# A non-local attention block on one NeuronCore: image loop written out, products placed at block ends, and the turned diagonal tiles of blocks 2 to 5 multiplied as halves

## The chip, the core and the metric

The kernel runs on one NeuronCore of a Trainium2 chip. TensorE (PE, its weight loads PEld) multiplies, VectorE (DVE), ScalarE (ACT) and GpSimd (POOL) work on tiles, and SyncE (SP) issues the DMAs. The engines run side by side and wait for each other on semaphores. The metric is the device time of one execution in microseconds; three executions of the kernel before gave 2091.82, 2092.5 and 2095.53 us, the median is 2092.5 us.

## The reference

```python
x = x + L(gn(x), g_w, g_b, W_w, W_b, gamma, beta)   # x: 4 images, 256 channels, 64 x 64
# inside L, for one image, with v = gn(x) as 256 x 4096:
g_x  = g_w @ v + g_b                    # 128 x 4096
f    = v.T @ v                          # 4096 x 4096, symmetric
attn = softmax(f, axis=-1)
y    = attn @ g_x.T                     # 4096 x 128
wy   = W_w @ y.T + W_b                  # 256 x 4096
# then a batch norm of wy over all four images, plus v
```

`gn` is a group norm with 32 groups. All of it is float32.

## The kernel before, in words

**Blocks and tiles.** The 4096 positions of an image are cut into NB = 8 blocks of 512. f is symmetric, so only the chunks (j, c) with c >= j are multiplied (`multiply`, L1280 to L1282): the operands are split into a high and a low part (`xh`, `xl`, in a rounded type called fp32r), and a product of 128 rows by 512 columns is six matmuls. VectorE takes it out of PSUM with the row maxima (L1067), and takes column maxima into `colmax` (L1075). A chunk stays in a slot of `ring` (or in a part of `fy_c` and `fy_d`) and is spilled to DRAM for later use.

**One step.** A block j of outputs is the sum over 32 tiles of 128 by 512, so an image has 8 x 32 = 256 steps, numbered 0 to 255; step 32 j + i is tile i of block j. A "right" tile comes from chunks (j, c) of the block itself. Its exponential is taken with the row maxima (ACT, L863), it is turned by four transposes of TensorE (`turn`, L1333, done two steps ahead) into one of two banks, cast to a high half `phi` by ScalarE (`split_hi`, L904, 3 buffers), its low half `plo` is made by VectorE (`split_lo`, L1098, 2 buffers), and TensorE multiplies with three fp32r matmuls (`attend`, L1361 to L1363). A "left" tile is a part of an earlier chunk that needs no turn: POOL subtracts the spread row maxima `maxrow` (L784), ScalarE takes the exponential (L883), VectorE adds it to the column sum `lacc` (L1109, L1113), and TensorE multiplies it in one full float32 matmul (L1357; the trace has two records for it). In blocks 1 to 6 the four tiles of the diagonal chunk (j, j) are taken as left tiles as well, straight from `ring`: the "turned diagonal tiles". Right tiles are the only ones that are split.

**Order.** Every engine has its own instruction stream, written by `step(b, s, ...)` for the steps in turn. In one step TensorE first turns the tile of step s + 2, then makes the products that `PRODUCT_STEP` puts at s, then multiplies tile s; after that come small transposes and projections. ScalarE makes in step s the exponential of the left tile of step s + 3, the high half for step s + 2, and then the exponentials of right tiles. VectorE makes the low half of step s, then sums, then takes the products. POOL goes through the left tiles in order, as far ahead as its data allow; at a block's start it waits for `maxrow` (L874 on ScalarE). `PRODUCTS_FROM` says at which step the products of block j begin. `plan_products` spreads them over a number of steps from there; the steps at which the maxima of a block are merged (`MERGE_STEP`) follow from the last product. From step `NEXT_AT` on, the first products of the next image are made, which need the next image's `xl` (POOL, L755).

**Images.** Images 0 to 3 follow each other. Step 12 of image 0 to step 11 of image 3 are one hardware loop over three rounds on every engine (`Fori`, on TensorE at L1483), in which each wait compares with a number computed from the loop's register; image 3 from step 12 on is written out.

Of the kernel before, what the change touches and what calls it, by code (L numbers as in the profile page):

```python
# [25 lines left out]
F32 = mybir.dt.float32  # L26
# [48 lines left out]
PRODUCTS_FROM = {j: (j - 1) * TPB for j in range(1, NB)} | {6: 5 * TPB - 8, 7: 5 * TPB + 8}  # L75
# [53 lines left out]
FULL = range(1, NB)  # L129
SPLIT = [p for p in range(TILES) if not (tile(p)[3] and p // TPB in FULL)]  # L130
# [37 lines left out]
def plan_products():  # L168
# [3 lines left out]
    for j in range(1, NB):  # L172
        n = T * (NB - j)
        steps = range(PRODUCTS_FROM[j], PRODUCTS_FROM[j] + {1: 22, 2: 19, 3: 18, 4: 18, 5: 18, 6: 2 * n, 7: 2 * n}[j])
# [85 lines left out]
NEXT_AT, NEXT_TO = XN_STEP[0] + 5, TILES - 18  # L260
# [145 lines left out]

def nonlocal_block(nc, x, wg, bg, ww, vec, out):
# [5 lines left out]
    with ExitStack() as ctx:  # L413
# [128 lines left out]
        lo_made = sem("lo_made")  # L542
        left_added = sem("left_added")
# [54 lines left out]
        def pool_subs(b, w):  # L598

            n = b * NLEFT + w  # L600
            return n - sum(v < w for v in VSUBS) if isinstance(b, int) and b == B - 1 else n
# [17 lines left out]
        def y_home(b, j):  # L619

            return colmax[:, j, :] if isinstance(b, int) and j < NB - 1 else yn[:, :]
# [6 lines left out]
        def _(sp):  # L628
# [94 lines left out]
            with sp.Fori(0, B - 1) as b:  # L723
# [21 lines left out]
        def _(pool):  # L745
# [16 lines left out]

            def image(b, more):
                for c in range(len(NEXT_G), NB):
                    make_gl(b, c)
                for w in range(NLEFT):
# [8 lines left out]

                    if not more and w in VSUBS:
                        continue
# [28 lines left out]
            with pool.Fori(0, B - 1) as b:  # L806
                image(b, True)
# [5 lines left out]
        def _(act):  # L813
# [53 lines left out]
            def take_maxrow(b, j):  # L867
# [4 lines left out]
                if isinstance(b, int) and b == B - 1 and VSUBS[0] < LEFT_OF[j][0]:  # L872
# [3 lines left out]
            def exp_left(b, p):  # L876

                w = LEFT_NO[p]
                if isinstance(b, int) and b == B - 1 and w in VSUBS:
# [31 lines left out]
            def take_inverse(b, j):  # L911

                act.wait_ge(inverse_spread, b * NB + j + 1)
                if j > 0:
                    if isinstance(b, int):
# [60 lines left out]
            with act.Fori(0, B - 1) as b:  # L976
# [27 lines left out]
        def _(dve):  # L1004
# [145 lines left out]
            def step(b, p, more, tail=False, first=False):  # L1150
                j, i = divmod(p, TPB)
                if p in SPLIT_NO:
                    split_lo(b, p, first)
# [55 lines left out]
            with dve.Fori(0, B - 1) as b:  # L1209
# [47 lines left out]
        def _(pe):  # L1257
            last_image = B - 1
# [60 lines left out]
            def turn(b, p, first=False):  # L1319
# [7 lines left out]
                if n >= 2:  # L1327
                    pe.wait_ge(lo_made, b * NSPLIT + SPLIT_NO[IN_PSUM[n - 2]] + 1)
                elif not first:
                    pe.wait_ge(lo_made, b * NSPLIT + SPLIT_NO[IN_PSUM[n - 2]] + 1 - NSPLIT)  # L1330
# [6 lines left out]
            def attend(b, p, first=False):  # L1337
# [6 lines left out]
                if p in SPLIT_NO:  # L1344
                    pe.wait_ge(lo_made, b * NSPLIT + SPLIT_NO[p] + 1)
                else:
                    w = LEFT_NO[p]
                    if w in LEFT_OF[j][:2]:
# [208 lines left out]
```

## Time and profile before

| what | value |
|---|---|
| median of three executions | 2092.5 us |
| the profiled execution's own time | 2091.74 us |
| its span, first to last instruction | 2090.0 us |
| TensorE busy | 2027.0 us, 97% |
| VectorE, ScalarE, GpSimd busy | 1543.7, 1110.8, 788.9 us |
| mean granted TensorE clock | 0.999 of full speed |
| TensorE idle before L1333, released by VectorE's low half | 15.1 us in 30 places |

A row of the timeline reads: start in us, length in us, engine, line, operation, output<-input, count, and in brackets the idle time before it and what ended it. Matmuls overlap, so the distance between the starts of two rows is what one costs, and the length of a row is not. Image 1's steps run from about 574.3 to 1072.0 us of the span and image 2's to 1571.5 us.

### The profile page before, as it was taken

What the parts mean: (1) busy time and instruction counts of PE and PEld (TensorE: products, weight loads), DVE (VectorE), ACT (ScalarE), POOL (GpSimd) and SP (SyncE); (2) the same over time, 40 slices, a digit from 0 to 9 for tenths busy, and PEclk for the clock granted to TensorE, in tenths of its full rate; (3) what the DMA queues carried; (4) which work ended last, traced back from release to release, by engine and by line L of the source; (5) the groups of instructions that cost most, each with busy time, mean ns of one, the idle gap of its engine ahead of it and who ended that gap; (6) DMA issues with size and microseconds to landing.
All of it is one profiled execution on the core that took longest, in us unless ns stands there. A gap on an engine that the chain in (4) does not pass through costs nothing.

```text
span 2090.0 us, 32328 instructions
## 1 busy us (share of the span) xinstructions
PE 2027.0 (97%) x9348; PEld 1453.2 (70%) x9348; DVE 1543.7 (74%) x3113; ACT 1110.8 (53%) x2312; POOL 788.9 (38%) x608
## 2 busy tenths in 40 slices
PE   5999999999999999999999999999999999999998
PEld 4787777666688777766678777766668877776443
DVE  5777777877777777787777677787777677777777
ACT  4345555566545445547553555546645544554656
POOL 4001233469601123458820122246970202344740
PEclk9999999999999999999999999999999999999999
DMA  3222334556411333565622223455551132346988
GB/s 126 112 90 87 106 117 126 177 165 207 163 68 72 121 101 104 160 201 158 215 82 82 82 94 129 131 177 161 186 187 66 66 121 94 99 131 200 338 297 346
DMA packets 107542, 300.29 MB, mean 144 GB/s; under 512 B 11488, under 2 KB 11872, under 8 KB 93536
## 3 DMA queue, kind: packets, MB, share of 16 engines
q1 hardware_dynamic: 107360, 298.11, 41.9%
q8 instruction: 84, 1.38, 0.3%
q14 instruction: 98, 0.80, 0.1%
HBM read 157.55 MB, written 140.51 MB: 143 GB/s over the span
## 4 chain that ended last, share of the span: by engine, by line
PE 75%; issue 8%; POOL 7%; DVE 4%; ACT 4%; DMA 1%; SPq 0%; ACTq 0%; DVEq 0%; POOLq 0%
PE bank L1357 13%; PE bank L1280 11%; PE bank L1282 11%; PE bank L1281 11%; PE bank L1333 8%; PE bank L1361 4%; PE bank L1363 4%; PE bank L1362 4%; PE bank L1516 3%; POOL fy_c L784 3%; POOL fy_d L784 3%; PE bank L1427 2%; ACT ring L863 2%; DVE plo L1098 1%; POOL xl L755 1%
## 5 line engine op out<-in xcount | busy, mean ns | idle before, releaser
L904 ACT CAST phi<-bank 128x512 fp32r<-128x512 f32 x480 | 281.3, 586 | 697.8 <-PE bank L1333 696.0
L1067 DVE TENSOR_SCALAR_CACHE_REDUCE ring<-bank 128x512 f32<-128x512 f32 x560 | 385.7, 690 | 269.0 <-PE bank L1282 197.5
L1280 PE MATMUL bank<-xh 128*128 128x512 f32 (+3 forms) x1152 | 513.8, 446 | 10.5 <-POOL xl L755 10.2
L1098 DVE TENSOR_TENSOR plo<-bank,phi 128x512 fp32r<-128x512 f32 x480 | 329.8, 687 | 153.4 <-ACT phi L904 107.3
L1282 PE MATMUL bank<-xh,xl 128*128 128x512 f32 (+3 forms) x1152 | 436.3, 379 | 0.0
L1281 PE MATMUL bank<-xl,xh 128*128 128x512 f32 (+3 forms) x1152 | 433.4, 376 | 0.0
L863 ACT ACTIVATE ring<-ring,nmax 128x512 f32<-128x512 f32 x464 | 334.2, 722 | 1.3
L784 POOL TENSOR_TENSOR fy_d<-fy_d,maxrow 128x512 f32<-128x512 f32 x181 | 234.6, 1299 | 254.8 <-DMA fy_d<-spill 254.8
L1333 PEld LDWEIGHTS bank<-ident,ring 128*128 128x128 f32 x1856 | 221.9, 140 | 150.4 <-issue 80.1
L784 POOL TENSOR_TENSOR fy_c<-fy_c,maxrow 128x512 f32<-128x512 f32 x192 | 248.1, 1295 | 175.3 <-DMA fy_c<-spill 175.1
L1333 PE MATMUL bank<-ident,ring 128*128 128x128 f32 x1856 | 281.3, 274 | 17.5 <-DVE plo L1098 15.1
L1280 PEld LDWEIGHTS bank<-xh 128*128 128x128 f32 x1152 | 217.8, 189 | 81.5 <-issue 34.9
L1075 DVE TENSOR_TENSOR colmax<-bank,colmax 128x512 f32<-128x512 f32 x392 | 269.0, 686 | 0.0
L1281 PEld LDWEIGHTS bank<-xl,xh 128*128 128x128 f32 x1152 | 218.7, 190 | 61.0 <-issue 32.7
L1282 PEld LDWEIGHTS bank<-xh,xl 128*128 128x128 f32 x1152 | 217.1, 188 | 41.6
L784 POOL TENSOR_TENSOR ring<-ring,maxrow 128x512 f32<-128x512 f32 x96 | 122.7, 1289 | 279.9 <-ACT maxrow L874 279.9
L1361 PE MATMUL bank<-phi,gh 128*128 128x512 f32 x480 | 217.1, 452 | 4.0 <-DVE plo L1098 3.8
L1357 PE MATMUL bank<-fy_c,gf 128*128 128x512 f32 x400 | 203.9, 594 | 2.5 <-DVE bank L1113 2.4
L1357 PE MATMUL bank<-fy_d,gf 128*128 128x512 f32 x376 | 191.3, 594 | 2.6 <-DVE bank L1113 2.6
L1363 PE MATMUL bank<-plo,gh 128*128 128x512 f32 x480 | 189.4, 395 | 0.0
L1362 PE MATMUL bank<-phi,gl 128*128 128x512 f32 x480 | 188.1, 392 | 0.0
L761 POOL TENSOR_TENSOR gl<-gf,gh 128x512 fp32r<-128x512 f32 x32 | 41.2, 1289 | 367.6 <-ACT gh L848 367.6
(152 smaller groups left out, 2765.2 us busy)
## 6 DMA issues: line engine op xcount, KB each, us to landing
spill<-ring SPq DMA_DIRECT2D x108, 1024.0 KB, 4.3
fy_c<-spill SPq DMA_DIRECT2D x200, 256.0 KB, 4.0
fy_d<-spill SPq DMA_DIRECT2D x188, 256.0 KB, 4.1
ring<-x_dram SPq DMA_DIRECT2D x42, 512.0 KB, 4.9
lbuf<-spill SPq DMA_DIRECT2D x60, 256.0 KB, 3.7
yd<-yn SPq DMA_DIRECT2D x24, 256.0 KB, 3.4
out_dram<-ring SPq DMA_DIRECT2D x10, 512.0 KB, 3.0
fx_a<-x_dram SPq DMA_DIRECT2D x8, 512.0 KB, 6.5
```

The lines of the kernel that those rows point to most:

```text
L784: nc.gpsimd.tensor_tensor(left_at(w), left_at(w), maxrow[:, :], ALU.subtract).then_inc(left_sub, 1)
L863: nc.scalar.activation(slot_tile(u, t), slot_tile(u, t), ACT.Exp, bias=nmax[:, j % 3, t:t + 1], accum_out=rsum[:, j % 2, t, c:c + 1]).then ...
L904: nc.scalar.copy(phi[:, HI_BUF[n], :], whole(p)).then_inc(hi_made, 1)
L1067: last = nc.vector.tensor_scalar(slot_tile(u, t), src, 1.0, None, ALU.mult, ALU.max, accum_out=rowm[:, t, c:c + 1])
L1098: nc.vector.tensor_tensor(plo[:, n % LOS, :], whole(p), phi[:, HI_BUF[n], :].bitcast(F32), ALU.subtract).then_inc(lo_made, 1)
L1280: nc.tensor.matmul(dst, xh[:, k, rows], xh[:, k, cols], start=(k == 0), stop=False)
L1281: nc.tensor.matmul(dst, xh[:, k, rows], xl[:, k, cols], start=False, stop=False)
L1282: last = nc.tensor.matmul(dst, xl[:, k, rows], xh[:, k, cols], start=False, stop=(k == K - 1))
L1333: last = nc.tensor.transpose(pps[:, n % 2, t * P:(t + 1) * P], slot_tile(u, t)[:, r * P:(r + 1) * P], ident[:, :])
L1357: nc.tensor.matmul(y, gf[:, c, r, :], left_at(LEFT_NO[p]), start=begin, stop=end).then_inc(tile_used, 1)
L1361: nc.tensor.matmul(y, gh[:, c, r, :], hi, start=begin, stop=False)
L1363: nc.tensor.matmul(y, gh[:, c, r, :], lo, start=False, stop=end).then_inc(tile_used, 1)
```

## The change

- The loop over the images is written out on all five engines: no branch, and every wait compares with a constant. `LastImage` only keeps image 3's special treatment.
- Products begin earlier in blocks 2, 3 and 5: from step 26, 60 and 124 instead of 32, 64 and 128 (six, four and four steps ahead of the block before's end), one in each step up to the old begin; those of block 1 are spread over 20 steps instead of 22. The last product of each block and its `MERGE_STEP` stay. The next image's first product moves from step 184 to 185, and many of the following by one step.
- The 16 turned diagonal tiles of blocks 2 to 5 (steps 66, 67, 70, 72; 98, 100, 102, 104; 129, 132, 134, 135; 161, 163, 165, 168) are split: ScalarE casts a high half from `ring`, POOL makes the low half (`make_self_lo`), TensorE multiplies three times. `phi` and `plo` keep 3 and 2 buffers, so a half waits for the split tile three or two places before it. In POOL's stream the low half of step p stands ahead of the subtraction of the first left tile after step p + 3 (`SELF_AT`). VectorE's low halves are those of right tiles alone, as before.

```diff
-PRODUCTS_FROM = {j: (j - 1) * TPB for j in range(1, NB)} | {6: 5 * TPB - 8, 7: 5 * TPB + 8}
+PRODUCTS_FROM = {j: (j - 1) * TPB for j in range(1, NB)} | {2: TPB - 6, 3: 2 * TPB - 4, 5: 4 * TPB - 4, 6: 5 * TPB - 8, 7: 5 * TPB + 8}
...
-FULL = range(1, NB)
-SPLIT = [p for p in range(TILES) if not (tile(p)[3] and p // TPB in FULL)]
+SELF = [p for p in LEFT if turned_self(*tile(p)[:2]) and 2 <= tile(p)[0] <= 5]
+SELF_AT = {p: min(w for w, q in enumerate(LEFT) if q > p + 3) for p in SELF}
+SPLIT = [p for p in range(TILES) if not tile(p)[3] or p in SELF]
...
-        steps = range(PRODUCTS_FROM[j], PRODUCTS_FROM[j] + {1: 22, 2: 19, 3: 18, 4: 18, 5: 18, 6: 2 * n, 7: 2 * n}[j])
+        steps = range(PRODUCTS_FROM[j], PRODUCTS_FROM[j] + {1: 20, 2: 25, 3: 22, 4: 18, 5: 22, 6: 2 * n, 7: 2 * n}[j])
...
-NEXT_AT, NEXT_TO = XN_STEP[0] + 5, TILES - 18
+NEXT_AT, NEXT_TO = XN_STEP[0] + 6, TILES - 18
...
+class LastImage(int):
+
+    pass
...
-            with sp.Fori(0, B - 1) as b:
+            for b in range(B - 1):
...
+            def make_self_lo(b, p):
+
+                n = SPLIT_NO[p]
+                pool.wait_ge(hi_made, b * NSPLIT + n + 1)
+                pool.wait_ge(tile_used, b * TILES + split_tile(n - LOS) + 1)
+                nc.gpsimd.tensor_tensor(plo[:, n % LOS, :], left_at(LEFT_NO[p]), phi[:, HI_BUF[n], :].bitcast(F32),
+                                        ALU.subtract).then_inc(self_lo_made, 1)
+
...
+                    for p in SELF:
+                        if SELF_AT[p] == w:
+                            make_self_lo(b, p)
                     if not more and w in VSUBS:
                         continue
                     j = tile(LEFT[w])[0]
...
-                if p in SPLIT_NO:
+                if p in PSUM_NO:
                     split_lo(b, p, first)
...
-                if n >= 2:
-                    pe.wait_ge(lo_made, b * NSPLIT + SPLIT_NO[IN_PSUM[n - 2]] + 1)
-                elif not first:
-                    pe.wait_ge(lo_made, b * NSPLIT + SPLIT_NO[IN_PSUM[n - 2]] + 1 - NSPLIT)
+                if n >= 2 or not first:
+                    pe.wait_ge(lo_made, b * len(IN_PSUM) + n - 1)
...
-                if p in SPLIT_NO:
-                    pe.wait_ge(lo_made, b * NSPLIT + SPLIT_NO[p] + 1)
+                if p in PSUM_NO:
+                    pe.wait_ge(lo_made, b * len(IN_PSUM) + PSUM_NO[p] + 1)
                 else:
                     w = LEFT_NO[p]
+                    if p in SELF:
+                        pe.wait_ge(self_lo_made, b * len(SELF) + SELF.index(p) + 1)
                     if w in LEFT_OF[j][:2]:
```

The other four engines' loops are changed like SP's.

TensorE's stream at the end of block 0, steps 27 and 28 in the loop's body before (L1333 turns, L1361 to L1363 multiply a right tile by its halves):

```order
L1333 MATMUL bank<-ident,ring 128x128 [waits lo_made,right_exp]
L1333 MATMUL bank<-ident,ring 128x128 x3
L1361 MATMUL bank<-phi,gh 128x512 [waits lo_made]
L1362 MATMUL bank<-phi,gl 128x512
L1363 MATMUL bank<-plo,gh 128x512
L1328 REGISTER_ALU [waits right_exp]
L1333 MATMUL bank<-ident,ring 128x128 [waits lo_made]
L1333 MATMUL bank<-ident,ring 128x128 x3
L1343 REGISTER_ALU
L1361 MATMUL bank<-phi,gh 128x512 [waits lo_made,gl_made]
```

and step 27 now (L1349 turns, L1298 to L1305 are product (2, 2, 1), L1379 to L1381 multiply):

```order
L1349 MATMUL bank<-ident,ring 128x128 [waits lo_made,right_exp]
L1349 MATMUL bank<-ident,ring 128x128 x3
L1298 MATMUL bank<-xh 128x384 [waits f_taken]
L1299 MATMUL bank<-xl,xh 128x384
L1300 MATMUL bank<-xh,xl 128x384
L1298 MATMUL bank<-xh 128x384
L1299 MATMUL bank<-xl,xh 128x384
L1300 MATMUL bank<-xh,xl 128x384
L1305 MATMUL bank<-ident,ring 128x128 [waits f_taken]
L1379 MATMUL bank<-phi,gh 128x512 [waits lo_made]
L1380 MATMUL bank<-phi,gl 128x512
L1381 MATMUL bank<-plo,gh 128x512
```

A product stands between the turn and the multiplication where there was none, and the register instructions are gone.

POOL's stream at the start of block 3 before (subtractions for steps 98, 99, 100 and 102, 103, 104, 106, 108; `ring` tiles are the turned diagonal ones):

```order
L784 TENSOR_TENSOR ring<-ring,maxrow 128x512 [waits maxrow_made]
L783 REGISTER_ALU
L784 TENSOR_TENSOR lbuf<-lbuf,maxrow 128x512 [waits loaded0]
L784 TENSOR_TENSOR ring<-ring,maxrow 128x512 x2
L783 REGISTER_ALU
L784 TENSOR_TENSOR fy_c<-fy_c,maxrow 128x512 [waits loaded1]
L784 TENSOR_TENSOR ring<-ring,maxrow 128x512
L784 TENSOR_TENSOR fy_d<-fy_d,maxrow 128x512 [waits loaded2]
L784 TENSOR_TENSOR fy_c<-fy_c,maxrow 128x512 [waits loaded3]
```

and now (L802 subtracts, L775 makes a low half, for steps 98, 100, 102 and 104 in turn):

```order
L802 TENSOR_TENSOR ring<-ring,maxrow 128x512 [waits maxrow_made]
L802 TENSOR_TENSOR lbuf<-lbuf,maxrow 128x512 [waits loaded0]
L802 TENSOR_TENSOR ring<-ring,maxrow 128x512
L775 TENSOR_TENSOR plo<-ring,phi 128x512 [waits tile_used,hi_made]
L802 TENSOR_TENSOR ring<-ring,maxrow 128x512
L802 TENSOR_TENSOR fy_c<-fy_c,maxrow 128x512 [waits loaded1]
L775 TENSOR_TENSOR plo<-ring,phi 128x512 [waits tile_used,hi_made]
L802 TENSOR_TENSOR ring<-ring,maxrow 128x512
L775 TENSOR_TENSOR plo<-ring,phi 128x512 [waits tile_used,hi_made]
L802 TENSOR_TENSOR fy_d<-fy_d,maxrow 128x512 [waits loaded2]
L775 TENSOR_TENSOR plo<-ring,phi 128x512 [waits tile_used,hi_made]
```

Four low halves, each with a wait for TensorE and ScalarE, now stand among the subtractions.

## Rows read from the trace of the kernel before

**Rows 1.** The page: span, and busy time of each engine.

```profile
span 2090.0 us, 32328 instructions
PE 2027.0 (97%) x9348; PEld 1453.2 (70%) x9348; DVE 1543.7 (74%) x3113; ACT 1110.8 (53%) x2312; POOL 788.9 (38%) x608
```

**Rows 2.** Windows, image 1 and 2: us, busy by engine, PEclk, DMA.

```profile
574.30:1072.00 497.70, 490.33 (x2304) 356.96 (x2304) 369.79 (x762) 266.90 (x568) 200.49 (x153) 1.00 0.40 132
1072.00:1571.50 499.50, 491.87 (x2304) 358.08 (x2304) 369.71 (x762) 266.84 (x568) 200.48 (x153) 1.00 0.40 131
```

**Rows 3.** The waits of PE: us in total, times, longest.

```profile
PE bank L1333 <- DVE plo L1098: 15.1, 30, 1.3
```

**Rows 4.** The loop's line L1483; timeline of PE after the branches; the clock there.

```profile
L1483 PEldq COMPARE_BRANCH  x3: 83/3422/3678, 615.6 to 1612.8; - x3
...
619.27 0.65 PE L1333 MATMUL bank<-ident,ring 128*128 128x128 f32 x4 [1.34 <-DVE plo L1098]
...
1117.21 0.65 PE L1333 MATMUL bank<-ident,ring 128*128 128x128 f32 x4 [1.60 <-issue]
...
1117.80:1121.20 3.40, 3.40 (x10) 2.63 (x9) 0.79 (x3) 1.30 (x3) 0.00 (x0) 0.50 0.35 131
```

**Rows 5.** Timeline of PE, column maxima for blocks 1 and 5, images 1 and 3.

```profile
654.24 0.60 PE L1394 MATMUL bank<-ident,colmax 128*128 128x128 f32 x4
...
894.56 0.60 PE L1394 MATMUL bank<-ident,colmax 128*128 128x128 f32 x4
...
1649.96 0.60 PE L1394 MATMUL bank<-ident,colmax 128*128 128x128 f32 x4
...
1889.32 0.60 PE L1394 MATMUL bank<-ident,colmax 128*128 128x128 f32 x4
```

**Rows 6.** Timeline of PE, end of block 0 in image 1, steps 27 to 29.

```profile
659.66 0.60 PE L1333 MATMUL bank<-ident,ring 128*128 128x128 f32 x4
...
660.79 0.60 PE L1333 MATMUL bank<-ident,ring 128*128 128x128 f32 x4
...
663.31 0.66 PE L1333 MATMUL bank<-ident,ring 128*128 128x128 f32 x4 [1.22 <-DVE plo L1098]
```

**Rows 7.** Timeline of PE, end of block 3 in image 1, steps 125 and 126.

```profile
854.89 0.60 PE L1333 MATMUL bank<-ident,ring 128*128 128x128 f32 x4
...
856.48 0.66 PE L1333 MATMUL bank<-ident,ring 128*128 128x128 f32 x4 [0.28 <-DVE plo L1098]
```

**Rows 8.** Timeline, step 184: the next image's first product.

```profile
949.74 2.36 POOL L755 TENSOR_TENSOR xl<-ring,xh 128x1024 fp32r<-128x1024 f32 x1 [1.70 <-ACT xh L834]
...
952.22 0.49 PE L1280 MATMUL bank<-xh 128*128 128x512 f32 x1 [1.49 <-POOL xl L755]
```

**Rows 9.** Timeline of PE in block 5: two left tiles, one right tile, a left tile.

```profile
922.50 1.02 PE L1357 MATMUL bank<-fy_c,gf 128*128 128x512 f32 x2
923.36 1.02 PE L1357 MATMUL bank<-ring,gf 128*128 128x512 f32 x2
...
926.46 0.40 PE L1361 MATMUL bank<-phi,gh 128*128 128x512 f32 x1
...
927.16 1.02 PE L1357 MATMUL bank<-fy_d,gf 128*128 128x512 f32 x2
```

**Rows 10.** Groups by shape: line, engine, tiles, count | busy us, mean ns | idle.

```profile
L784 POOL TENSOR_TENSOR ring<-ring,maxrow 128x512 f32<-128x512 f32 x96 | 122.7, 1289 | 279.9 <-ACT maxrow L874 279.9
L904 ACT CAST phi<-bank 128x512 fp32r<-128x512 f32 x480 | 281.3, 586 | 697.8 <-PE bank L1333 696.0
L761 POOL TENSOR_TENSOR gl<-gf,gh 128x512 fp32r<-128x512 f32 x32 | 41.2, 1289 | 367.6 <-ACT gh L848 367.6
```

**Rows 11.** Timeline, block 3's start: POOL, then PE at steps 100 and 102.

```profile
796.32 1.28 POOL L784 TENSOR_TENSOR ring<-ring,maxrow 128x512 f32<-128x512 f32 x1 [12.80 <-ACT maxrow L874]
...
810.58 1.02 PE L1357 MATMUL bank<-ring,gf 128*128 128x512 f32 x2
...
813.00 1.02 PE L1357 MATMUL bank<-ring,gf 128*128 128x512 f32 x2
```

More of the change, by code:

```diff
@@ L542, in nonlocal_block @@
         lo_made = sem("lo_made")
+        self_lo_made = sem("self_lo_made")
         left_added = sem("left_added")
@@ L600, in pool_subs @@
             n = b * NLEFT + w
-            return n - sum(v < w for v in VSUBS) if isinstance(b, int) and b == B - 1 else n
+            return n - sum(v < w for v in VSUBS) if b == B - 1 else n
         def kept(u, h):
@@ L619, in y_home @@
         def y_home(b, j):
-            return colmax[:, j, :] if isinstance(b, int) and j < NB - 1 else yn[:, :]
+            return colmax[:, j, :] if b == B - 1 and j < NB - 1 else yn[:, :]
         def whole(p):
@@ L805, in _ @@
                 make_gl(0, c)
-            with pool.Fori(0, B - 1) as b:
+            for b in range(B - 1):
                 image(b, True)
@@ L871, in take_maxrow @@
                     act.wait_ge(left_sub, pool_subs(b, LEFT_OF[j][0]))
-                if isinstance(b, int) and b == B - 1 and VSUBS[0] < LEFT_OF[j][0]:
+                if b == B - 1 and VSUBS[0] < LEFT_OF[j][0]:
                     act.wait_ge(left_sub_v, sum(v < LEFT_OF[j][0] for v in VSUBS))
@@ L878, in exp_left @@
                 w = LEFT_NO[p]
-                if isinstance(b, int) and b == B - 1 and w in VSUBS:
+                if b == B - 1 and w in VSUBS:
                     act.wait_ge(left_sub_v, VSUBS.index(w) + 1)
@@ L914, in take_inverse @@
                 if j > 0:
-                    if isinstance(b, int):
+                    if b == B - 1:
                         act.wait_ge(y_made, b * NB + j)
@@ L975, in _ @@
                 step(0, s, True, first=True)
-            with act.Fori(0, B - 1) as b:
+            for b in range(B - 1):
                 for s in range(HEAD, TILES):
@@ L1208, in _ @@
                 step(0, p, True, first=True)
-            with dve.Fori(0, B - 1) as b:
+            for b in range(B - 1):
                 for p in range(HEAD, TILES):
@@ L1257, in _ @@
         def _(pe):
-            last_image = B - 1
+            last_image = LastImage(B - 1)
             def average(n, stage, first=False):
@@ L1365, in shared_free @@
             def shared_free(n, kind, j, h=0):
-                order = SHARED[not isinstance(n, int)]
+                order = SHARED[not isinstance(n, LastImage)]
                 at = next(q for q, use in enumerate(order) if use[1:] == (kind, j, h))
@@ L1482, in _ @@
                 step(0, p, True, first=True)
-            with pe.Fori(0, B - 1) as b:
+            for b in range(B - 1):
                 for p in range(HEAD, TILES):
@@ L1499, in final_wy @@
                         elif u == 1:
-                            pe.wait_ge(lo_made, B * NSPLIT)
+                            pe.wait_ge(lo_made, B * len(IN_PSUM))
                         elif u == 2:
```

## The prediction

> **What bounds the kernel now.** I read the page first: TensorE is busy 97% of a span of 2090.0 us, while VectorE, ScalarE and GpSimd stand at 74%, 53% and 38% [rows 1]. So a microsecond counts if it is taken off TensorE's own work or out of one of its gaps, and not otherwise. The windows by image say the same for the middle of the program: 490.33 of 497.70 us busy in image 1, and image 2 is 1.8 us longer with the same work [rows 2]. The waits of TensorE name the gaps: 15.1 us before its transposes, 30 times, for a low half that VectorE made late [rows 3], and once an image a product waits for `xl` [rows 8]. The chain of waits has POOL's subtractions in it, but in blocks 2 to 5 TensorE has next to no gap behind them, so they are cover, not the bound.
>
> The sum below is made against the profiled execution: span 2090.0 us, its own time 2091.74 us, 1.7 us around the span. The median of the runs shown is 2092.5 us, 0.8 us more.
>
> **Part 1, the loop written out.** TensorE's branch takes 3.42 and 3.68 us in the two passes that go back, and 0.08 us where the loop ends [rows 4]. Matmuls already queued hide half of it; what shows is 1.34 us before the next transpose in the first pass and 1.60 us in the second. After the second the granted clock is at half (0.50, the 1.2 GHz level) for 3.40 us, in which TensorE was busy throughout; that is 1.7 us of work lost, and it is the 1.8 us by which image 2 is longer [rows 2, 4]. Together 4.6 us. The pauses of the other engines are under TensorE's. Lower bound of this term: nothing, if the straight code pauses elsewhere; upper: 5 us.
>
> Where the Trainium skill prices this, it gives a compare-and-branch about 108 ns ("Advanced Engine Details and Errata", Control Flow Timing), which would make this term some 0.2 us in all. The row that lasts 3.42 us disagrees, and the exit of 0.08 us agrees. The same skill says that a taken branch to code that is not at hand forces a fetch ("Runtime: NRT & Kernel Launch", Instruction fetch mechanics), which is how I read the two long ones.
>
> The register instructions before waits go too. Image 3, already written out, shows what they cost: from the column maxima for block 1 to those for block 5 image 1 needs 894.56 - 654.24 = 240.32 us, image 3 needs 1889.32 - 1649.96 = 239.36 us [rows 5], 0.96 us less over half an image. Three images make 2.9 us. A part of it is in gaps that part 2 counts, and a part may be image 3's lack of loads for a next image, so I take 2.0; bounds 0 and 5.9 (both halves of three images).
>
> **Part 2, products at block ends.** At the end of block 0 ScalarE has four right exponentials and the copy of `maxrow` beside its casts, and TensorE only turns and multiplies. Its turns of steps 28 and 29 start at 660.79 and 663.31, 2.52 us apart, those of 27 and 28 only 1.13 us (660.79 - 659.66) [rows 6], so 1.4 us are lost, in each image. Now products stand in steps 26, 27 and 28 ahead of that turn, four us of TensorE's work (a full product is six matmuls of 0.23 us, a third of the 0.70 us that three half matmuls take [rows 9]), so the gap should close: 4 x 1.4 = 5.6 us. At the end of block 3 the same distance is 856.48 - 854.89 = 1.59 us [rows 7], 0.46 us lost, and products in 124 and 125 stand ahead of it: 4 x 0.46 = 1.8 us. In block 1 the long gap is at the turn of step 60, which is issued ahead of the product of step 60: it stays, and I count only the short ones of steps 61 to 63, 0.2 us an image, 0.8 us.
>
> What do the moved products leave behind? Steps 38 to 42, 68 to 72 and some of 129 to 143 now have none. Those stretches mix left and right tiles, and in the trace the like stretches (steps 83 to 92) run without a gap, since a left tile needs no turn and no cast. I take 0. The product's takes on VectorE and its spill on SP move with it; a right step at a block end then has three operations on VectorE, against 1.13 + 1.4 = 2.5 us of TensorE, and VectorE has a quarter of its time free [rows 1]. Bound: if ScalarE's backlog is only pushed on, all 8.2 us stay lost.
>
> The next image's first product waits 1.49 us for `xl`, which ends at 952.1 [rows 8]. Put one step later, it lets the left tile of that step go first, 0.86 us; three images, 2.6 us. Bounds 0 and 4.
>
> **Part 3, the diagonal tiles as halves.** Two full tiles start 923.36 - 922.50 = 0.86 us apart, three half matmuls take 927.16 - 926.46 = 0.70 us [rows 9]. So a tile gains 0.16 us, and 64 of them 10.2 us. ScalarE gets 64 casts of 586 ns, 38 us on an engine with 47% to spare. POOL gets 64 low halves; the trace has the same subtraction, with the rounded output, at 1289 ns, no different from a plain one [rows 10]: 83 us on an engine at 38%.
>
> The price is in the waits, since a low half can begin only when TensorE has finished the split tile two places back (`plo` has 2 buffers), and then needs 1.29 us and about 0.1 us of signals. Block 3 worked out: the subtractions begin at 796.32 and follow each other every 1.25 us; the low half for step 98 slips between them, the one for step 102 waits for step 100 to be finished (810.58 + 0.86 = 811.44). In between TensorE has the right tile of step 101 and a projection, and would reach step 102 at 813.00 [rows 11]: 1.56 us for 1.39 us, no wait. But then POOL has a subtraction and the next low half in turn, 2.5 us, where TensorE has a split tile (0.70), a turn (1.13 - 0.70 = 0.43) and a left tile (0.86), 2.0 us: 0.5 us of waiting at step 104. Walked through in this way block 2 waits 0.3 us (step 72, only step 71 between it and 70), block 4 0.4 us and block 5 0.1 us, and ScalarE's extra casts delay a turn in block 3 by 0.2 us. That is 1.5 us an image, 6.0 us in all, which leaves 4.2 us of the 10.2. Behind a late low half on POOL stand the subtractions of the next left tiles; in block 5 they come up to 6 us later than now, but POOL, busy 200 of 498 us in an image [rows 2], runs ahead of ScalarE at other places and makes it good. Bounds: no wait at all (10.2 us gained), and a wait of 0.3 us at each of the 64 (9 us lost).
>
> **Sum.** 4.6 + 2.0 + 5.6 + 1.8 + 0.8 + 2.6 + 4.2 = 21.6 us. Span 2090.0 - 21.6 = 2068.4 us; with 1.7 us around it and 0.8 us to the median, **2071 us**.
>
> **Rivals.**
> - *The gaps at block ends move instead of closing* (ScalarE's backlog, or gaps where products left). For it: the gap's cause is ScalarE, which gets no less work, and more after step 64. Against it: ScalarE idles 696 us waiting for turns [rows 10]. Time 2071 + 8.2 = 2079 us.
> - *The low halves are never late, and constants help all through.* For it: POOL ran ahead in most of block 2. 2071 - 6 - 3.9 = 2061 us.
> - *The branch's pause stays, as pauses in the fetch of straight code.* For it: there is more code; against it: image 3, written out, shows none. 2071 + 4.6 = 2076 us. By the skill's 108 ns for a branch the result would be 2075 us.
> - *Slower:* the low half on POOL comes late at each of the 64 tiles, because it can't start before the split tile two back is done and only one half tile (0.70 us) lies between: 1.39 - 0.70 = 0.7 us each, 44.8 us. Without part 3's 4.2 us and with its 10.2 us the rest gains 27.6 us, so from 0.43 us a tile on the kernel is slower; at 0.7 us it takes 2092.5 + 17 = 2110 us. Against it: between most of the pairs lie two or more steps or a product of 1.4 us.
> - *Part 2 and 3 do nothing together* and only the loop is gained, with some new waits: about 2088 us, within 0.2%.
>
> **How the numbers follow.** Forecast 50%, gaps move 18%, never late 16%, branch stays 6%, nothing but the loop 5%, slower 5%. The time is that of the likeliest, 2071 us. The range goes from 2060, the never-late case, to 2083, gaps that move together with half of the halves' bound; it leaves out the last two cases and the far ends of the others. 0.2% (4 us) is about what a measurement of this kernel can tell from no change. Faster needs less than 2088.3 us: 0.91; same 0.04; slower 0.05.
>
> **What would show it.** In the profile after: the turns of steps 28 and 29 with a product between them and no idle before the second; no gap of over 1 us near the old loop ends and a clock of 1.00 throughout; the wait for `xl` near 0.6 us; in block 3 a gap of about half a us before the three half matmuls of step 104, released by POOL's `plo`; POOL busy about 83 us more and ScalarE 38 us; TensorE's busy time smaller by about 10 us. The prediction is wrong if TensorE's waits for POOL's `plo` add up to over 10 us, or if gaps appear in steps 38 to 42 and 68 to 72.

## The result and the profile after

The changed kernel takes 2071.3 us (median of 4 runs, 2067.2 to 2072.7) where the kernel before took 2092.2 us beside it (2090.3 to 2095.5): a ratio of 0.9895, 95% interval 0.9876 to 0.9915. The forecast was 2071 us. The profiled execution took 2067.2 us and is the quickest of the four, so its trace shows some 4 us more gain than the median; where these come from is said below.

The page, span and busy time by engine, to be held against [rows 1]:

```profile
span 2064.3 us, 28577 instructions
PE 2010.7 (97%) x9412; PEld 1463.6 (71%) x9412; DVE 1539.2 (75%) x3113; ACT 1153.2 (56%) x2376; POOL 868.6 (42%) x672
```

64 more matmuls, casts and subtractions stand here, and 3,751 fewer instructions in all: the register instructions and branches. GpSimd has 79.7 us more, ScalarE 42.4 us. TensorE's busy time is 16.3 us less. By the prediction's count 10 us of it are the halves; the rest is, as I read it, time in which matmuls had run longer behind gaps and at the lower clock.

The windows of images 1, 2 and 3, columns as in [rows 2]:

```profile
569.00:1060.20 491.20, 486.35 (x2320) 359.72 (x2320) 369.42 (x761) 277.25 (x583) 220.31 (x169) 1.00 0.41 133
1060.20:1551.80 491.60, 486.52 (x2321) 359.77 (x2320) 369.40 (x761) 277.30 (x583) 220.31 (x169) 1.00 0.40 133
1551.80:2000.10 448.30, 439.76 (x2081) 318.83 (x2082) 336.29 (x660) 252.68 (x542) 183.07 (x143) 1.00 0.45 156
```

Images 1 and 2 are 6.5 and 7.9 us shorter than in [rows 2] and now alike. The 1.8 us by which image 2 was longer fit the stretch at half clock (granted clock 0.50 in [rows 4], 1.00 throughout here).

TensorE's waits (us in total, times, longest), to be held against [rows 3]:

```profile
PE bank L1349 <- DVE plo L1116: 10.6, 17, 1.5
PE bank L1298 <- POOL xl L762: 5.8, 1, 5.8
PE bank L1379 <- DVE plo L1116: 3.6, 9, 0.7
PE bank L1379 <- POOL plo L775: 2.3, 8, 0.4
```

And GpSimd's own wait before its 64 low halves:

```profile
POOL plo L775 <- PE bank L1381: 107.8, 28, 11.3
```

The waits before transposes (line 1349, before 1333) are down from 30 to 17, but the longest is now 1.5 us. Eight waits of 0.2 to 0.4 us for GpSimd's low halves are new. The one wait for `xl` that is left is the start of the program. Only 28 of the 64 low halves begin after a wait for TensorE to give a buffer back; before the other 36 GpSimd has no idle time, it comes to them from its own queue.

Timeline of TensorE at the end of block 0, the turns of steps 28 to 30 and the products before them (compare [rows 6]), then at step 184 of image 1 (compare [rows 8]):

```profile
661.06 0.60 PE L1349 MATMUL bank<-ident,ring 128*128 128x128 f32 x4
...
662.66 0.39 PE L1300 MATMUL bank<-xh,xl 128*128 128x512 f32 x1
...
663.58 0.60 PE L1349 MATMUL bank<-ident,ring 128*128 128x128 f32 x4
...
666.10 0.60 PE L1349 MATMUL bank<-ident,ring 128*128 128x128 f32 x4
...
940.03 1.12 PE L1375 MATMUL bank<-fy_d,gf 128*128 128x512 f32 x2 [0.27 <-DVE bank L1131]
941.21 0.50 PE L1298 MATMUL bank<-xh 128*128 128x512 f32 x1
```

The turns still stand 2.52 us apart, but now with a product between them and no idle before any. At step 184 the 1.49 us in front of the product are 0.27 us in front of a left tile plus about 0.3 us that the product starts late (941.21 - 940.03 - 0.86).

The new waits of image 1, at step 72 and at step 104, on TensorE's timeline and then on GpSimd's:

```profile
747.68 0.40 PE L1381 MATMUL bank<-plo,gh 128*128 128x512 f32 x1
748.43 0.50 PE L1379 MATMUL bank<-phi,gh 128*128 128x512 f32 x1 [0.36 <-POOL plo L775]
...
805.29 1.02 PE L1375 MATMUL bank<-fy_c,gf 128*128 128x512 f32 x2
806.53 0.50 PE L1379 MATMUL bank<-phi,gh 128*128 128x512 f32 x1 [0.22 <-POOL plo L775]
806.87 0.39 PE L1380 MATMUL bank<-phi,gl 128*128 128x512 f32 x1
```

```profile
747.10 1.28 POOL L775 TENSOR_TENSOR plo<-ring,phi 128x512 fp32r<-128x512 f32 x1 [1.16 <-PE bank L1381]
...
802.72 1.29 POOL L775 TENSOR_TENSOR plo<-ring,phi 128x512 fp32r<-128x512 f32 x1 [0.64 <-PE bank L1381]
803.96 1.30 POOL L802 TENSOR_TENSOR fy_d<-fy_d,maxrow 128x512 f32<-128x512 f32 x1
805.21 1.27 POOL L775 TENSOR_TENSOR plo<-ring,phi 128x512 fp32r<-128x512 f32 x1
```

Two kinds of lateness are to be seen. At step 72 GpSimd itself stands idle for 1.16 us until TensorE gives a buffer back. At step 104 it works without a pause: low half, subtraction, low half. The idle time that the row prints understates a gap, since the first matmul behind one also takes longer: at step 104 the left tile starts at 805.29 and would be through at 806.15, which is 0.38 us before 806.53, and the next matmul comes 0.34 us later in place of 0.23. Together 0.49 us. In the same way step 72 loses 0.63 us.

One gap stands where no part of the change seems to be, in the step that begins each of the images 1 to 3. TensorE and ScalarE, image 1:

```profile
568.60 0.40 PE L1381 MATMUL bank<-plo,gh 128*128 128x512 f32 x1
570.54 0.63 PE L1349 MATMUL bank<-ident,ring 128*128 128x128 f32 x4 [1.55 <-DVE plo L1116]
```

```profile
569.09 0.59 ACT L922 CAST phi<-bank 128x512 fp32r<-128x512 f32 x1 [1.01 <-PE bank L1381]
```

The cast waits for the last tile of the image before to be finished. `phi` has three buffers, taken in turn by the number of the split tile within the image. With 120 split tiles the turn closes at the image's end; with 136, which is not a multiple of three, tiles 135 and 0 use the same buffer back to back. From 568.83 (568.60 + 0.23) to 570.54 are 1.71 us.

### The profile page after: what moved, and what is told of

Read it like the earlier page. It is cut to its first block, busy times and chain, and to the rows that moved or that the text cites. A ratio compares the mean times of both kernels' runs of the same rounds, so it can differ in the third digit from the quotient of the medians.

```text
span 2064.3 us, 28577 instructions
## 1 busy us (share of the span) xinstructions
PE 2010.7 (97%) x9412; PEld 1463.6 (71%) x9412; DVE 1539.2 (75%) x3113; ACT 1153.2 (56%) x2376; POOL 868.6 (42%) x672
## 4 chain that ended last, share of the span: by engine, by line
PE 87%; POOL 3%; DVE 3%; ACT 3%; issue 2%; DMA 1%; SPq 0%; DVEq 0%; ACTq 0%; POOLq 0%
PE bank L1375 15%; PE bank L1298 12%; PE bank L1300 12%; PE bank L1299 12%; PE bank L1349 9%; PE bank L1379 6%; PE bank L1381 5%; PE bank L1380 5%; PE bank L1534 3%; PE bank L1445 2%; PE bank L1305 1%; PE bank L1333 1%; PE bank L1334 1%; ACT phi L922 1%; DVE plo L1116 1%
## 5 line engine op out<-in xcount | busy, mean ns | idle before, releaser
L1298 PE MATMUL bank<-xh 128*128 128x512 f32 (+3 forms) x1152 | 508.6, 442 | 6.2 <-POOL xl L762 5.8
L1349 PEld LDWEIGHTS bank<-ident,ring 128*128 128x128 f32 x1856 | 224.1, 140 | 125.6 <-issue 67.5
L1349 PE MATMUL bank<-ident,ring 128*128 128x128 f32 x1856 | 279.4, 273 | 11.3 <-DVE plo L1116 10.6
L802 POOL TENSOR_TENSOR fy_d<-fy_d,maxrow 128x512 f32<-128x512 f32 x177 | 230.2, 1303 | 139.6 <-DMA fy_d<-spill 139.5
L802 POOL TENSOR_TENSOR fy_c<-fy_c,maxrow 128x512 f32<-128x512 f32 x192 | 248.1, 1296 | 79.0 <-DMA fy_c<-spill 79.0
L1298 PEld LDWEIGHTS bank<-xh 128*128 128x128 f32 x1152 | 217.5, 189 | 73.6 <-issue 26.6
L1379 PE MATMUL bank<-phi,gh 128*128 128x512 f32 x544 | 247.4, 455 | 6.1 <-DVE plo L1116 3.6
L1381 PE MATMUL bank<-plo,gh 128*128 128x512 f32 x544 | 214.2, 394 | 0.0
L1380 PE MATMUL bank<-phi,gl 128*128 128x512 f32 x544 | 212.8, 391 | 0.0
L802 POOL TENSOR_TENSOR ring<-ring,maxrow 128x512 f32<-128x512 f32 x96 | 122.8, 1286 | 211.4 <-ACT maxrow L892 211.4
```

The source lines that it names most:

```text
L802: nc.gpsimd.tensor_tensor(left_at(w), left_at(w), maxrow[:, :], ALU.subtract).then_inc(left_sub, 1)
L1298: nc.tensor.matmul(dst, xh[:, k, rows], xh[:, k, cols], start=(k == 0), stop=False)
L1349: last = nc.tensor.transpose(pps[:, n % 2, t * P:(t + 1) * P], slot_tile(u, t)[:, r * P:(r + 1) * P], ident[:, :])
L1379: nc.tensor.matmul(y, gh[:, c, r, :], hi, start=begin, stop=False)
L1380: nc.tensor.matmul(y, gl[:, c, r, :], hi, start=False, stop=False)
L1381: nc.tensor.matmul(y, gh[:, c, r, :], lo, start=False, stop=end).then_inc(tile_used, 1)
```

## The experiments

Each median is held against the kernel before, run beside it (2093.2 to 2093.4 us in each group).

**1 to 3: one part of the change left out, or one alone.** `e1_loop_only` is the changed kernel with the old product steps and `SELF = []`; `e2_no_halves` has `SELF = []` alone, `e3_no_products` the old product steps alone:

```diff
-SELF = [p for p in LEFT if turned_self(*tile(p)[:2]) and 2 <= tile(p)[0] <= 5]
+SELF = []
-... | {2: TPB - 6, 3: 2 * TPB - 4, 5: 4 * TPB - 4, 6: 5 * TPB - 8, ...
+... | {6: 5 * TPB - 8, ...
-{1: 20, 2: 25, 3: 22, 4: 18, 5: 22, ...
+{1: 22, 2: 19, 3: 18, 4: 18, 5: 18, ...
-NEXT_AT, NEXT_TO = XN_STEP[0] + 6, TILES - 18
+NEXT_AT, NEXT_TO = XN_STEP[0] + 5, TILES - 18
```

> Only the loop over the images is written out; the table of products, the next image's first step and the full float32 diagonal tiles are those of before. My theory: the two long branches (1.34 and 1.60 us of TensorE shown, and 1.7 us of work lost at half clock) and the register instructions go, 4.6 + 2.0 us, so about 2086 us (ratio 0.997), image 2 as long as image 1, no clock drop, and the first half of each image as long as image 3's was (240.3 us becomes 239.4 us between the column maxima of blocks 1 and 5). Rival, pauses of the fetch stay in straight code: no change, 2092 us. Rival, nearly all of the 21 us comes from the loop: 2075 us.

> The changed kernel with the diagonal tiles of blocks 2 to 5 full again (no low halves on POOL, no casts for them), loop written out and products moved. My theory: the halves give 10.2 us of TensorE's work less some 6 us of waits, so this is 4 us slower than the changed kernel, about 2075 us. And a thing that the profile of the changed kernel shows: the turn in step 0 of images 1 to 3 waits 1.74 us instead of 0.70; if that is due to the number of split tiles (136 is not a multiple of the 3 phi buffers, so that the last and the first split tile of two images share one; 120 is a multiple), it is back at 0.7 us here. Rival, the halves do nothing or cost: 2071 us or less. Rival, the wait at an image's start is due to the straight code: it stays at 1.74 us.

> The changed kernel with the products at their old steps (blocks 2, 3 and 5 begin at 32, 64 and 128, block 1 over 22 steps, next image from step 184). My theory: 5.6 + 1.8 + 0.8 + 2.6 = 10.8 us slower than the changed kernel, about 2082 us, with a gap of 1.3 to 1.4 us at the turn of step 29 in each image, 0.4 us at step 126 and over 1.4 us before the next image's first product. Rival, the gaps had only moved: within 2 us of the changed kernel. Rival, the low halves need the moved products as cover: more than 15 us slower, with waits for POOL's plo well over 0.5 us in blocks 2 and 5.

Measured: 2084.8 us (ratio 0.9959, 0.9946 to 0.9973); 2070.6 us (0.9894, 0.9879 to 0.9909); 2083.3 us (0.9953, 0.9939 to 0.9966). The loop alone is worth 8.6 us. The products are worth 14.2 us without halves (2084.8 - 2070.6) and 12.0 us with them (2083.3 - 2071.3). By image the products are worth the same with and without halves: image 1 takes 494.9 us in both kernels with the old steps, 491.2 and 491.1 us in the two with the new ones. So the 2.2 us between 14.2 and 12.0 us are not the halves' but the spread between runs; the spans of the profiled executions give 11.7 us without halves and 14.6 us with them. The halves bring nothing: 2070.6 us without, 2071.3 us with. So the expectation for the time of `e2_no_halves` missed, and the question was where their 4 us went; its guess about the turn in step 0 held, the wait there is back at 0.6 us.

Here and below, the length of a step is measured from the last matmul of one tile to that of the next. Between `e1_loop_only` and the kernel before, the step with the branch (step 12) differs by 1.5 us in image 1 and by 3.3 us in image 2, the branch with the stretch at half clock behind it. Another 1.2 and 1.6 us an image are spread over many turns. From the column maxima of block 1 to those of block 5 `e1_loop_only` needs 239.4 to 239.6 us, as image 3 did before [rows 5].

**4: the seam between two images.** `e4_seam` lets the sequence of `phi` buffers repeat one buffer in the middle of a long run of left tiles, where there is time, so that it closes at the image's end:

```diff
-HI_BUF = [n % HIS for n in range(NSPLIT)]
+REPEAT_AT = max(n for n in range(1, NSPLIT) if SPLIT[n] - SPLIT[n - 1] > 20)
+HI_BUF = [(n - (n >= REPEAT_AT)) % HIS for n in range(NSPLIT)]
```

> The changed kernel with one edit: the order of the three phi buffers repeats one buffer in block 7, between the split tiles of steps 224 and 253, where 28 steps lie between, so that the last and first split tiles of two images no longer share one. Theory that the wait at an image's start comes from the shared buffer: the turn in step 0 waits 0.7 instead of 1.74 us, three images, 2.5 to 3.1 us faster, about 2068 us. Rival, the wait is due to ScalarE's backlog of exponentials there: no change, 2071 us.

Measured: 2066.9 us (0.9871, 0.9856 to 0.9886). Timeline of its TensorE at the same place, image 2:

```profile
1058.42 0.40 PE L1382 MATMUL bank<-plo,gh 128*128 128x512 f32 x1
1059.25 0.63 PE L1350 MATMUL bank<-ident,ring 128*128 128x128 f32 x4 [0.43 <-DVE plo L1117]
```

The gap is 0.60 us here (1059.25 - 1058.42 - 0.23) and 1.71 us in the changed kernel: 1.1 us an image, 3.3 us. The medians of the two differ by 4.5 us with intervals that overlap; the rows carry the verdict. With the seam mended, the halves are worth 3.8 us (2070.6 - 2066.9), against 4.2 us in the prediction. Against `e2_no_halves`, image 1 is 1.1 us shorter, and all of it lies in blocks 4 (0.7 us) and 5 (0.5 us): blocks 2 and 3, with half of the tiles, lose in waits what the halves save.

**5: the order of GpSimd's queue.** Seam mended, and the low half of step 104 made right behind that of step 102:

```diff
+SELF_AT[104] = SELF_AT[102]
```

> The seam's repeated cast buffer as before, and GpSimd makes the low half for step 104 right behind the one for step 102; the row subtraction that stood between them comes after. My theory of the 0.5 us gap at step 104 is the order of GpSimd's queue, so the gap should go, four images, 2 us: 2065 us against 2067 us. The rival, that the two low-half buffers set it, as they do at step 72, leaves the gap and 2067 us. The gap of 0.6 us at step 72 stays by both.

Measured: 2075.1 us (0.9913, 0.9900 to 0.9927), 8 us slower than `e4_seam` by the medians; the profiled spans, 2070.1 us and 2065.3, are 4.8 us apart. Timeline of GpSimd, ScalarE and TensorE there:

```profile
804.91 1.29 POOL L777 TENSOR_TENSOR plo<-ring,phi 128x512 fp32r<-128x512 f32 x1 [0.23 <-ACT phi L924]
806.15 1.29 POOL L804 TENSOR_TENSOR fy_d<-fy_d,maxrow 128x512 f32<-128x512 f32 x1
...
807.47 0.63 ACT L903 ACTIVATE fy_d<-fy_d 128x512 f32<-128x512 f32 x1 [1.92 <-POOL fy_d L804]
...
808.47 0.72 ACT L883 ACTIVATE ring<-ring,nmax 128x512 f32<-128x512 f32 x1
...
809.34 0.66 PE L1351 MATMUL bank<-ident,ring 128*128 128x128 f32 x4 [1.64 <-ACT ring L883]
```

The wait at step 104 is gone, so it was the queue's order and not the buffers. But the subtraction that was put back is awaited by ScalarE, behind whose exponential stands the right exponential of the tile that TensorE turns next: step 105 is 1.9 us longer than in `e4_seam` and step 104 0.5 us shorter, in four images 5.5 us. The rest of the 8 us between the medians isn't accounted for.

**6: VectorE makes the low halves.** The seam's sequence is kept, and `make_self_lo` moves, unchanged, from GpSimd's list to VectorE's step:

```diff
-                    for p in SELF:
-                        if SELF_AT[p] == w:
-                            make_self_lo(b, p)
+                if p in SELF:
+                    make_self_lo(b, p)
```

> The 64 low halves of the diagonal tiles are made by VectorE, in its own order, and not by GpSimd; the seam's repeated buffer is kept. If GpSimd's 1.29 us is what makes them late, the gaps at steps 72 and 104 shrink (4 x 1.1 us at most) and the time is 2063 to 2066 us. The rival: VectorE, with some 45 us more, is late for the low halves of turned tiles near those places, and the time is 2068 us or more.

Measured: 2091.3 us (0.9992, 0.9983 to 1.0001), the whole gain of the change gone. TensorE's waits for these low halves, and their group:

```profile
PE bank L1379 <- DVE plo L1114: 18.2, 20, 2.4
```

```profile
L1114 DVE TENSOR_TENSOR plo<-ring,phi 128x512 fp32r<-128x512 f32 x64 | 65.0, 1015 | 0.0
```

The longest of them, and GpSimd's timeline beside it:

```profile
1356.09 5.19 DVE L1114 TENSOR_TENSOR plo<-ring,phi 128x512 fp32r<-128x512 f32 x1
```

```profile
1355.74 1.28 POOL L792 TENSOR_TENSOR fy_c<-fy_c,maxrow 128x512 f32<-128x512 f32 x1
1356.99 1.28 POOL L792 TENSOR_TENSOR fy_d<-fy_d,maxrow 128x512 f32<-128x512 f32 x1
1358.24 1.26 POOL L792 TENSOR_TENSOR fy_c<-fy_c,maxrow 128x512 f32<-128x512 f32 x1
1359.47 1.26 POOL L792 TENSOR_TENSOR fy_d<-fy_d,maxrow 128x512 f32<-128x512 f32 x1
```

A usual one, with GpSimd's instructions around it:

```profile
304.14 1.30 POOL L792 TENSOR_TENSOR fy_d<-fy_d,maxrow 128x512 f32<-128x512 f32 x1
304.76 1.24 DVE L1114 TENSOR_TENSOR plo<-ring,phi 128x512 fp32r<-128x512 f32 x1
305.39 1.75 POOL L792 TENSOR_TENSOR fy_c<-fy_c,maxrow 128x512 f32<-128x512 f32 x1
```

The time is worse than both sides said, and not where the rival put it: the wait is for these low halves themselves. Their length isn't the reason, since 1015 ns as a mean are less than GpSimd's 1290. But VectorE has no idle time before any of the 64 (0.0 in the row of the group): it comes to them late, behind its other work. How much of the 24 us is this order and how much the stretched instructions wasn't separated.

One such subtraction takes 0.67 to 0.69 us in the 29 places where GpSimd does nothing meanwhile. In six it starts ahead of GpSimd's instruction and takes as little. In the 29 others it starts while one of GpSimd's is under way, and in 28 of them it ends 0.55 to 0.59 us after that one has ended, as above (304.76 + 1.24 = 306.00, and 304.14 + 1.30 = 305.44); GpSimd's next one, where it follows at once, takes about 1.75 us in place of 1.3. Once it took 5.19 us: it ends at 1361.28, 0.55 us after the last of four subtractions of GpSimd (1359.47 + 1.26 = 1360.73).

**7: the suspected cost doubled.** Seam mended; each low half on GpSimd is computed a second time into the same buffer.

```diff
                 nc.gpsimd.tensor_tensor(plo[:, n % LOS, :], left_at(...), phi[:, HI_BUF[n], :] ...).then_inc(self_lo_made, 1)
+                pool.wait_ge(self_lo_made, 2 * (b * len(SELF) + SELF.index(p)) + 1)
+                nc.gpsimd.tensor_tensor(plo[:, n % LOS, :], left_at(...), phi[:, HI_BUF[n], :] ...).then_inc(self_lo_made, 1)
```

> Each of the 64 low halves on GpSimd is computed twice into the same buffer, one after the other: the suspected cost is doubled (about 1.3 us more each, 83 us in all on GpSimd), the result is the same. By the theory that a low half can't begin before the split tile two places back is done, most of the 64 come late, by about 0.8 us as a mean: 2067 + 50 = 2117 us, within 2095 to 2135. The rival, that GpSimd has slack at most places and only steps 72 and 104 and one or two more are tight: 8 x 1.3 = 10 us, 2077 us.

Measured: 2136.9 us (1.0209, 1.0195 to 1.0223), just above the range given. The waits:

```profile
PE bank L1383 <- POOL plo L779: 58.0, 40, 2.8
```

70 us for 64 low halves that come 1.3 us later: 1.1 us of each 1.3 as a mean. But it doesn't show evenly. TensorE waits at ten of the 16 tiles of each image, for 0.2 to 0.4 us at steps 161 and 163 and for 2.0 to 2.8 us at steps 132, 135 and 165, more than the 1.3 us that one low half was delayed. In block 4 GpSimd works without a pause from one doubled low half to the next, so the delays add up in its queue. Its second subtraction for step 135, the wait for it, and the granted clock right behind:

```profile
891.28 1.27 POOL L779 TENSOR_TENSOR plo<-ring,phi 128x512 fp32r<-128x512 f32 x1
892.60 0.50 PE L1383 MATMUL bank<-phi,gh 128*128 128x512 f32 x1 [2.44 <-POOL plo L779]
893.40:896.60 3.20, 3.20 (x9) 2.51 (x8) 0.40 (x1) 0.63 (x1) 3.20 (x4) 0.50 0.48 152
```

Four such stretches at half clock stand behind long waits, some 7 of the 70 us. The experiment shows that the schedule has little room; it doesn't show that each low half was just in time before, and the step of 1.3 us is too coarse to tell how much room each had.

**8: the four tiles at the waits left whole.** No seam edit is needed, since 132 is a multiple of three:

```diff
-SELF = [p for p in LEFT if turned_self(*tile(p)[:2]) and 2 <= tile(p)[0] <= 5]
+SELF = [p for p in LEFT if turned_self(*tile(p)[:2]) and 2 <= tile(p)[0] <= 5 and p not in (67, 72, 104, 165)]
```

> Four of the 16 diagonal tiles (steps 67, 72, 104 and 165) are left whole: those at which, or right behind which, TensorE waits. The 132 split tiles that stay are a multiple of three, so the cast buffers don't repeat at the seam either. Sixteen halves fewer lose 16 x 0.15 = 2.4 us; the waits at steps 68, 72, 104 and 165 go, 4 x (0.14 + 0.62 + 0.49 + 0.12) = 5.5 us: 2064 us. If the waits only move to the next split tile, the time is 2067 to 2069 us.

Measured: 2066.6 us (0.9875, 0.9858 to 0.9891), the same as `e4_seam` by the medians. In its trace no wait of TensorE for GpSimd's low halves is left, where `e4_seam` has eight (2.3 us); a gap of 0.2 us at the turn of step 105 is new, and image 2 is 0.5 us shorter (489.9 us against 490.4). Expected were 0.8 us an image (5.5 - 2.4 us in four); the traces show 0.3 to 0.5 us in images 0 to 2. The new gap takes 0.2 us of the difference, the rest is open.

**9: the next image's products one step later again,** on top of experiment 8.

```diff
-NEXT_AT, NEXT_TO = XN_STEP[0] + 6, TILES - 18
+NEXT_AT, NEXT_TO = XN_STEP[0] + 7, TILES - 18
```

> The kernel with twelve halved tiles, and the next image's first product one step later again (7 steps behind the first normalised chunk in place of 6). One step took the wait for xl from 1.7 to 0.9 us; by my reading (a left tile of 0.86 us goes first) the second step takes the rest: three images, 2.6 us, 2064 us against 2066.6 us. The rival, that VectorE's or GpSimd's later work for those products becomes late by the same step: 2066 to 2068 us.

Measured: 2066.4 us (0.9877, 0.9862 to 0.9892), no gain. The rival holds. The 0.3 us in front of the first product are gone, and gaps open where the same products stand closer together, at the end of block 5 and in block 6; image 1 is 0.7 us longer than in experiment 8 (490.3 us against 489.6). Timeline of TensorE in block 6:

```profile
961.22 1.02 PE L1375 MATMUL bank<-fy_c,gf 128*128 128x512 f32 x2
962.67 0.50 PE L1298 MATMUL bank<-xh 128*128 128x512 f32 x1 [0.43 <-DVE colmax L1093]
```

**10: block 2's products back at step 32,** seam mended, the other product steps new.

```diff
-PRODUCTS_FROM = ... | {2: TPB - 6, 3: 2 * TPB - 4, ...
+PRODUCTS_FROM = ... | {3: 2 * TPB - 4, ...
-{1: 20, 2: 25, 3: 22, 4: 18, 5: 22, ...
+{1: 22, 2: 19, 3: 22, 4: 18, 5: 22, ...
```

> The changed kernel with the repeated cast buffer at the seam, but the products of block 2 begin at step 32 again and not at 26. The prediction priced this edit at 5.6 us (the turn of step 29 alone): 2066.9 + 5.6 = 2072.5 us. The traces of the kernels with the old product steps show three gaps in block 0 (steps 20, 29, 31), 2.05 us an image: 2066.9 + 8.2 = 2075 us. Nothing: 2067 us.

Measured: 2075.0 us (0.9915, 0.9901 to 0.9928), 8.1 us more than `e4_seam`. That is what the traces had said. But the edit has two parts, since it also spreads block 1's products over 22 steps again, and the expectation priced both as block 2's. The trace tells them apart. The gap at the turn of step 20 lies ahead of every product of block 2 and can only come from block 1's spread (products of steps 13 and 17 stand at 14 and 18 again); the gap at step 29 is block 2's:

```profile
638.71 0.63 PE L1350 MATMUL bank<-ident,ring 128*128 128x128 f32 x4 [0.26 <-DVE plo L1117]
...
658.48 0.63 PE L1350 MATMUL bank<-ident,ring 128*128 128x128 f32 x4 [1.12 <-DVE plo L1117]
```

Up to step 23 each image is 0.5 us longer than in `e4_seam`, 2.0 us in all, and from step 24 to 47 1.5 us, 6.0 us in all. No gap stands at step 31 here.

**11: the products alone, the loop kept:** the kernel before with the three edited lines of numbers.

```diff
-PRODUCTS_FROM = ... | {6: 5 * TPB - 8, ...
+PRODUCTS_FROM = ... | {2: TPB - 6, 3: 2 * TPB - 4, 5: 4 * TPB - 4, 6: 5 * TPB - 8, ...
-{1: 22, 2: 19, 3: 18, 4: 18, 5: 18, ...
+{1: 20, 2: 25, 3: 22, 4: 18, 5: 22, ...
-NEXT_AT, NEXT_TO = XN_STEP[0] + 5, TILES - 18
+NEXT_AT, NEXT_TO = XN_STEP[0] + 6, TILES - 18
```

> The kernel before with its loop kept and without the halves, with the new product steps alone. If the parts add up, the loop is worth 8.6 us here too (the step from before to the loop written out alone): 2070.6 + 8.6 = 2079 us, and the product steps are worth 14 us. If the products close only what the loop's register instructions left open, it is 2083 us or more.

Measured: 2076.5 us (0.9926, 0.9912 to 0.9939). Beside `e2_no_halves` the loop is worth 5.9 us here, not 8.6. TensorE's timeline after the two branches, and then the windows of images 1 and 2 and of the stretch behind the second branch:

```profile
615.08 0.65 PE L1333 MATMUL bank<-ident,ring 128*128 128x128 f32 x4 [1.38 <-DVE plo L1098]
1109.07 0.65 PE L1333 MATMUL bank<-ident,ring 128*128 128x128 f32 x4 [1.70 <-issue]
```

```profile
570.10:1063.80 493.70, 489.06 (x2304) 357.27 (x2304) 370.20 (x762) 267.15 (x568) 200.26 (x153) 1.00 0.40 133
1063.80:1557.80 494.00, 489.04 (x2304) 357.26 (x2304) 370.15 (x762) 267.13 (x568) 200.20 (x153) 1.00 0.40 133
1109.50:1113.00 3.50, 3.50 (x18) 2.84 (x16) 1.78 (x4) 1.30 (x3) 0.00 (x0) 1.00 0.41 157
```

The branches cost 1.4 and 1.7 us as in [rows 4], but the clock stays at 1.00 behind the second, and images 1 and 2 are alike. So the 1.7 us at half clock don't belong to every kernel that has this loop; why the clock fell in the one and not in the other isn't shown.

## Why the prediction was right, and where its terms were off

- **The loop, 6.6 us.** 8.6 us alone, 5.9 us with the new product steps in both kernels: the term lies between. Alone, the branches with the clock are 4.8 us (4.6 foretold) and what is spread over the images nearly 4 us (2.0 foretold). With the new product steps they are 3.5 us, since the clock didn't fall, and some 2 us. That the spread part is the register instructions is likely, as the counts of matmuls and of VectorE's instructions are the same in both, but wasn't tested by itself. The rival that the pause stays in straight code is out: no gap stands at the old ends of the loop. The clock's share (1.7 us) is shown for the kernel before only.
- **Products, 10.8 us.** 12.0 us with the halves, 14.2 without. The largest term, 5.6 us at the end of block 0, came out near 6.0 us (experiment 10). What the sum lacked is a term for block 1's products, whose spread over 20 steps in place of 22 was given no price: it closes the gap at the turn of step 20, 2.0 us. The terms of blocks 1 and 3 (0.2 and 0.46 us an image) come to 0.3 and 0.6 us between `e2_no_halves` and `e1_loop_only`. That the gaps would only move is refuted: nothing opened in steps 38 to 42. In steps 68 to 72, the other stretch that the prediction named as a sign of being wrong, two gaps stand, 0.14 us at step 68 and 0.6 us at step 72. Both come with the halves and not from moved products (`e2_no_halves` has neither). The gap at the turn of step 60 stayed, as foretold.
- **The wait for xl, 2.6 us.** At step 184 it fell by about the 0.86 us that were counted. Experiment 9 shows the limit: one step more brings nothing.
- **Halves, 4.2 us.** The prediction takes 10.2 us less waits of 1.5 us an image. The waits came to nearly 1.6 us: 0.1 at step 68, 0.6 at step 72 (0.3 foretold), 0.5 at step 104 (0.5), 0.2 at steps 101 and 102 (0.2, foretold at a turn, found as two delays within the multiplications), none in block 4 (0.4) and 0.1 at step 165 (0.1). That the sum is right is luck in part: block 2 lost more than was forecast and block 4 nothing. Both mechanisms, the buffer at step 72 and the queue at 104, are in the rows, and experiment 5 confirms the second. What the walk left out is the cast's buffers: it followed `plo` with its two and took `phi` with its three as it was, though the number of split tiles went from 120 to 136. That cost 3.3 us, and the halves as they were made brought nothing. The total was met because the products, and the loop, brought more than was forecast and the halves nothing: 8.6 + 14.2 - 0.7 = 22.1 us, against 6.6 + 10.8 + 4.2 = 21.6. So the time was met in part by luck.
- **Waits for GpSimd's low halves over 10 us** would have made the prediction wrong: they are 2.3 us. The rival that the halves are never late is out, and so is the slower one. Its condition, a low half that can start only when the tile two places back is done, is met for 28 of the 64. The margin is small all the same: experiment 7 shows that 1.3 us more on each low half costs 70 us.
- **The 4 us between the profiled run and the median.** In the last image VectorE takes some of the row subtractions, and they collide with GpSimd's or not. Its subtractions (min/median/max ns), in the changed kernel and in `e2_no_halves`:

```profile
L1138 DVE TENSOR_TENSOR fy_c<-fy_c,maxrow x8: 681/742/1641, 1939.8 to 1986.1; 128x512 f32<-128x512 f32 x8
```

```profile
L1138 DVE TENSOR_TENSOR fy_c<-fy_c,maxrow x8: 793/1416/1721, 1940.5 to 1990.3; 128x512 f32<-128x512 f32 x8
```

Image 3 takes 448.3 us in the one and 452.2 in the other, while images 1 and 2 differ by 0.2 us at most. That this sets the spread between runs of one kernel (5.5 us in the changed one) is my reading; it wasn't tested by itself.

## What to carry to other kernels

When a change alters how many times a ring of buffers is used in one pass of a loop, check that the count is still a multiple of every ring's size, also of those that the change doesn't touch. Give every edited number a term in the sum: the two steps by which block 1's products were drawn together had none, and were worth a third of the largest term. Before work is moved to an engine because that engine is idle, look at who waits for what is queued behind it: GpSimd was busy 42% of the time, and 1.3 us more in each low half cost 1.1 us as a mean.

## What the runs showed of the hardware

In experiment 6 a VectorE subtraction with both inputs in SBUF took 0.67 to 0.69 us by itself. Where one of GpSimd was under way, it ended 0.55 to 0.59 us after that one (28 of 29 times, at most 1.72 us long), and once after four that ran back to back (5.19 us). With one input in PSUM it took 0.67 to 0.69 us in all 480 cases, 157 of them beside a GpSimd instruction. The Trainium skill ("Trainium Architecture — The Big Picture", What this means for kernel authors) calls the port pair of VectorE and GpSimd an exclusive lock and not a split of bandwidth. The trace agrees: one engine's instruction is stretched by the other's, and GpSimd's next one is stretched in turn (1.75 us in place of 1.3). It adds that VectorE once let four GpSimd instructions pass; why it got in behind one elsewhere and not there isn't shown.
